# Gated attention rebuilt: decay matrix as one bf16 product of 94 rows, running maximum by a scan, tiles in an unrolled pipeline

## The reference, cut to what matters

```python
ig = x3 @ Wi + bi ; fg = x3 @ Wf + bf            # x3 = [q, k, v]; one value per position and head
log_f = log_sigmoid(fg)
cum = cumsum(log_f over positions)
log_D[s, t] = cum[s] - cum[t] + ig[t]  for t <= s, else -inf
max_log_D[s] = max over t of log_D[s, t]
D = exp(log_D - max_log_D)
C = (q @ k.T / 4) * D
Cn = C / (max(|C.sum(-1)|, exp(-max_log_D)) + 1e-6)
h = Cn @ v ; per head: h = (h - mean) * rsqrt(var + 1e-6) * ln_scale
x = x + h
```

## Time and profile before

| | us |
|---|---|
| median of 3 runs (lowest, highest) | 2200.45 (2195.76, 2201.08) |
| the profiled execution, its own time | 2195.36 |
| its span, first to last instruction | 2193.7 |
| the changed stage in it, first to last instruction | 761.3 to 1148.8 |
| mean granted TensorE clock over the span | 0.834 |

### The profile page before, as it was taken

The page is one execution under the profiler, slowest core; times in us unless marked ns, Lnnn a source line. Parts: engine busy times, 40 slices in busy tenths (PEclk is TensorE's granted clock), DMA queues, the critical chain, the costliest instruction groups (busy, mean ns, idle before and its releaser), DMA issues. The chain is left out here.

```text
span 2193.7 us, 34574 instructions
## 1 busy us (share of the span) xinstructions
PE 1514.8 (69%) x11413; PEld 938.5 (43%) x11458; DVE 1441.1 (66%) x2920; ACT 1114.8 (51%) x1540; POOL 570.7 (26%) x910
## 2 busy tenths in 40 slices
PE   3349999999399758787754575559999954776111
PEld 3326555555277634444421233335555542444000
DVE  6648888886245337667765999825555556775796
ACT  4517777777112124343444788723333334777454
POOL 3412333333200132322231344200010001111663
PEclk9999999999599969888985566569999977788555
DMA  5643555554200032112101000011010120000211
GB/s 168 196 108 86 136 131 131 134 131 95 80 1 0 4 75 48 43 45 62 34 7 60 0 1 1 1 39 35 25 34 23 27 82 20 1 1 1 48 48 39
DMA packets 94834, 120.62 MB, mean 55 GB/s; under 512 B 26128, under 2 KB 78552, under 8 KB 90108
## 3 DMA queue, kind: packets, MB, share of 16 engines
q1 hardware_dynamic: 94716, 119.12, 21.2%
HBM read 79.30 MB, written 22.09 MB: 46 GB/s over the span
## 5 line engine op out<-in xcount | busy, mean ns | idle before, releaser
L610 DVE TENSOR_REDUCE ratt_nmax<-ratt_psS 128x2 f32<-128x512 f32 x512 | 318.2, 683 | 92.9 <-PE ratt_psS L502 92.5
L576 ACT ACTIVATE ratt_E<-ratt_psT 128x1024 f32<-128x1024 f32 x256 | 255.0, 1023 | 106.0 <-PE ratt_psT L524 106.0
L502 PE MATMUL ratt_psS<-ratt_K,ratt_Q 72*128 72x256 bf16 x1024 | 204.3, 284 | 39.0 <-DMA ratt_K<-context_parts 33.6
L524 PE MATMUL ratt_psT<-ratt_Q,ratt_K 75*128 75x256 bf16 x1024 | 195.9, 275 | 5.5 <-DMA ratt_Q<-ratt_rows 5.2
L537 PE MATMUL ratt_psO<-ratt_E,ratt_V 128*32 128x256 f32 x2048 | 137.9, 387 | 0.7 <-ACT ratt_E L576 0.7
L502 PEld LDWEIGHTS ratt_psS<-ratt_K,ratt_Q 72*128 72x128 bf16 x1024 | 79.9, 99 | 135.1 <-issue 64.8
L524 PEld LDWEIGHTS ratt_psT<-ratt_Q,ratt_K 75*128 75x128 bf16 x1024 | 99.5, 98 | 23.5 <-DMA ratt_Q<-ratt_rows 5.6
L1355 PE MATMUL gatt_psA<-gatt_DA,gatt_same 128*128 128x512 f32 x128 | 89.3, 787 | 28.9 <-DVE gatt_DB L1240 25.3
L1174 POOL TENSOR_TENSOR gatt_DA<-gatt_own,gatt_a 128x1024 f32<-128x1024 f32 x32 | 61.6, 1937 | 143.8 <-PE gatt_psA L1358 90.6
L3302 PE MATMUL final_psT<-final_identh,final_Z 128*128 128x128 f16 x64 | 8.3, 310 | 110.4 <-ACT final_Z L3336 110.4
L1238 DVE TENSOR_REDUCE gatt_mx<-gatt_psA 128x16 f32<-128x1024 f32 x32 | 39.0, 1219 | 65.4 <-PE gatt_psA L1358 64.7
(11 more groups left out here) (461 smaller groups left out, 4000.3 us busy)
## 6 DMA issues: line engine op xcount, KB each, us to landing
ratt_Q<-z_parts SPq DMA_DIRECT2D x32, 576.0 KB
ratt_K<-context_parts SPq DMA_DIRECT2D x96, 192.0 KB
gatt_V<-in_ctx_dram SPq DMA_DIRECT2D x16, 512.0 KB, 6.2
z_parts<-prep_ZS SPq DMA_DIRECT2D x48, 128.0 KB, 2.7
context_parts<-prep_CS SPq DMA_DIRECT2D x48, 128.0 KB, 2.3
head_sums<-ratt_O SPq DMA_DIRECT2D x64, 72.0 KB
all_X<-in_x_dram SPq DMA_DIRECT2D x8, 512.0 KB
prep_C<-in_ctx_dram SPq DMA_DIRECT2D x8, 512.0 KB
```

The source lines that it names most:

```text
L502: mm = nc.tensor.matmul(psS[:, RING[h], c * D:(c + 1) * D], Q9[0:R, buf, h, k % 2, c * P:(c + 1) * P], K9[0:R, buf, h, k % 2, :], start=Tr ...
L524: mm = nc.tensor.matmul(psT[:, p % 2, e, c, :], K9[0:RM, buf, h, u, c * P:(c + 1) * P], Q9[0:RM, buf, h, u, :], start=True, stop=True)
L576: nc.scalar.activation(E[:, 2 * b + p // 2, 2 * (p % 2):2 * (p % 2) + 2], psT[:, p % 2], ACT.Exp, scale=SCALE).then_inc(exped, 1)
L610: nc.vector.tensor_reduce(nmax[:, k % 2, h, :], psS[:, RING[h]].rearrange("p (c t) -> p c t", c=2), AX.X, ALU.max, negate=True).then_inc(m ...
```

## The change

1. The diagonal spread on POOL, its f32 product, the separate mask product, the maximum over psA and the subtraction go. Instead a tile's exponent comes from one bf16 product per half of the heads, with 94 rows to contract (`decay`): 64 rows of an identity pattern against the mask, 24 rows for minus the running maximum of 8 heads in three bf16 parts, 6 rows for `a` of the two sequences in three bf16 parts. ACT's exponential reads psA and writes PB; DVE's `weigh` multiplies PB in place.
2. Per group PE transposes `a` to 64 partitions (group tile and head) x 128 positions (`turn_a`), DVE runs a maximum scan over each sequence (`running_maximum`), PE transposes the maximum back (`turn_maximum`, `take_maximum`), POOL splits `a` and minus the maximum into three bf16 parts (`split_rows`, five instructions on 64 x 256), SP writes them to DRAM in one DMA, waits for it, and reads them into the operands in five (`decay_rows`). These are double-buffered.
3. All engines run 44 unrolled slots (one per tile, 12 to fill and drain). In slot n = 4g + i, group g is prepared, tile t = n - 6 gets decay and exponential, tile t-1 is scored and weighed, tile t-2 is turned and multiplied by the values; the tail of group g-3 is done at i = 0, 1, 2.
4. The tail's Ln, Exp and Newton step become one POOL power on 128 x 64 (`power`); `tail` is 15 steps instead of 19. `sq` shares the memory of Z; `cen` is doubled. The gates read CT directly, so one DMA of 512 KB a group (`context`) goes. Keys are issued one half at a time, around `decay_rows` and the values' DMAs.

```diff
-                def spread_a(g, i):
-                    t = g * G + i
-                    pe.wait_ge(da_done, t + 1)
-                    pe.wait_ge(a_taken, t)
-                    for half in range(2):
-                        nc.tensor.matmul(psA[:, half, :], same[:],
-                                         DA[:, i % 2, half * HC:(half + 1) * HC, :].rearrange("p h t -> p (h t)"),
-                                         start=True, stop=False)
-                        mm = nc.tensor.matmul(psA[:, half, :], identb[:], mask[:].rearrange("p h t -> p (h t)"),
-                                              start=False, stop=True)
-                    mm.then_inc(a_spread, 1)
+                def decay(t):
+                    g, j = at(t)
+                    w = g % 2
+                    if j == 0:
+                        pe.wait_ge(rows_in[w], (g // 2 + 1) * ROWS_IN)
...
+                    if t > 0:
+                        pe.wait_ge(d_done, t)
+                    for c in range(KC):
+                        mm = nc.tensor.matmul(psA[:, c, :], LT[0:ROWS, w, j, c].rearrange("p u t -> p (u t)"),
+                                              R[0:ROWS, w, j, c].rearrange("p h t -> p (h t)"), start=True, stop=True)
+                    mm.then_inc(decayed, 1)
...
+                def decay_rows(g):
+                    w = g % 2
+                    sp.wait_ge(split, g + 1)
...
+                    sp.dma_start(rows_dram[w].rearrange("n p h t -> h n p t"), parts[:]).then_inc(rows_out, 16)
+                    sp.wait_ge(rows_out, g * 16 + 16)
...
+                    for p in range(3):
+                        sp.dma_start(LT[MX_ROW + p * HC:MX_ROW + (p + 1) * HC, w].rearrange(
+                            "h j c u t -> h (j c) (u t)"), rows_dram[w, 1, p].rearrange(
+                                "(x h) t -> h x t", h=HC)).then_inc(rows_in[w], 16)
+                    for u in range(2):
+                        for_u = rows_dram[w, 0].rearrange("p h (u t) -> u p h t", u=2)[u]
+                        sp.dma_start(R[A_ROW + 3 * u:A_ROW + 3 * u + 3, w].rearrange("p j c h t -> p (j c h) t"),
+                                     for_u).then_inc(rows_in[w], 16)
...
+                def power(g):
+                    pool.wait_ge(t_steps, g * TPER + 13)
+                    gp.tensor_tensor(tw[:, 9].rearrange("p j h -> p (j h)"), tw[:, 8].rearrange("p j h -> p (j h)"),
+                                     half[:], ALU.pow).then_inc(powered, 1)
...
+                for g in range(NG + 3):
                     if is_group(g + 1):
                         norm.on_pool(pool, g + 1)
+                    if is_group(g - 3):
+                        power(g - 3)
                     if is_group(g):
+                        split_rows(g)
+                    if is_group(g - 3):
+                        add(g - 3)
...
+                def running_maximum(g):
+                    step = Steps(dve, pair_steps, PPER, g)
+                    dve.wait_ge(a_turned, g + 1)
...
+                    step(v.tensor_copy(pair[:, 0], psG[0:GH, 0:P]))
+                    for u in range(2):
+                        x = pair[:, 0, u * L:(u + 1) * L]
+                        step(v.tensor_tensor_scan(pair[:, 2, u * L:(u + 1) * L], x, x, LOW, ALU.max, ALU.max))
+                    step(v.tensor_scalar(pair[:, 1], pair[:, 2], -1.0, None, ALU.mult))
...
+                for n in range(SLOTS):
+                    g, i = at(n)
+                    if i == 0:
+                        if is_group(g):
+                            front_gates(g)
+                        if is_tile(n - 7):
+                            weigh(n - 7)
+                        if is_group(g - 3):
+                            tail_centre(g - 3)
                     if i == 1:
+                        if is_group(g):
+                            front_logs(g)
+                        if is_tile(n - 7):
+                            weigh(n - 7)
+                        if is_group(g + 1):
+                            norm.take_stats(dve, g + 1)
+                        if is_group(g):
+                            front_sums(g)
+                        if is_group(g - 3):
+                            tail_variance(g - 3)
+                    if i == 2:
+                        if is_group(g):
+                            running_maximum(g)
+                        if is_tile(n - 7):
+                            weigh(n - 7)
+                        if is_group(g + 1):
+                            if is_group(g):
+                                dve.wait_ge(z_turned, g * KC + KC)
+                            norm.normalise(dve, g + 1, Z)
+                        if is_group(g - 3):
+                            tail_scale(g - 3)
                     if i == 3:
+                        if is_group(g):
+                            take_maximum(g)
+                        if is_tile(n - 7):
+                            weigh(n - 7)
...
+                for n in range(SLOTS):
+                    g, i = at(n)
+                    t = n - 6
+                    if is_group(g) and i == 1:
+                        running_sums(g)
+                    if is_tile(t):
+                        decay(t)
+                    if is_group(g) and i == 2:
+                        turn_a(g)
+                    if is_group(g) and i == 3:
+                        turn_maximum(g)
+                    if is_tile(t - 2):
+                        tg, tj = at(t - 2)
+                        heads.turn(pe, tg, tj)
+                    if is_group(g + 1) and i == 3:
+                        turn_z(g + 1, 0)
+                    if is_tile(t - 1):
+                        tg, tj = at(t - 1)
+                        heads.scores(pe, tg, tg % 3, tj)
+                    if is_group(g + 1) and i == 3:
+                        turn_z(g + 1, 1)
+                    if is_tile(t - 2):
...
+                        heads.values(pe, tg, tg % 2, tj)
+                    if is_group(g + 1) and i == 3:
+                        gates_of(g + 1)
...
+                for n in range(SLOTS):
+                    g, i = at(n)
+                    t = n - 6
+                    if is_group(g) and i == 0:
+                        softplus(g)
+                    if is_tile(t - 2):
+                        tg, tj = at(t - 2)
+                        heads.copy_turned(act, tg, tj)
+                    if is_tile(t):
+                        exp(t)
+                    if is_group(g + 1) and i == 3:
+                        query(g + 1, 0)
+                        query(g + 1, 1)
+                    if is_group(g - 3) and i == 0:
+                        tail(g - 3)
+                    if is_group(g - 1) and i == 1:
+                        place_values(g - 1)
+                    if is_tile(t - 2):
+                        take_output(t - 2)
```

More of the change, by code:

```diff
@@ L1062, in gated_attention @@
         lscale = s.sb("lscale", [P, D])
[L1063 to L1065 removed]
+        tri = s.sb("tri", [P, P])
         one = s.sb("one", [P, 1])
+        half = s.sb("half", [P, GH])
         Z = s.sb("Z", [P, G, D])
[L1068 removed]
         V2 = s.sb("V2", [P, BG, D])
@@ L1110, in _, with rows_of_context @@
                 c_dram = io["ctx_2048"].rearrange("b t d -> t b d")
-                def context(at):
-                    sp.dma_start(CG[:], CT[:, :, bass.ds(at, G * P)]).then_inc(cg_in, 16)
-                def rows_of_context(b0):
+                def rows_of_context(g):
                     for hp in range(2):
[L1117 to L1123, removed]
-                    if is_group(g + 1):
[L1125 to L1134, removed]
@@ new lines, in keys @@
+                def keys(g, half):
+                    after = g * G - 2 + 2 * half
+                    if after > 0:
+                        sp.wait_ge(heads.scored, after)
+                    for c in range(KC):
+                        for h in range(HC):
+                            rows = slice(h * DH, (h + 1) * DH)
+                            first = g * (G * P) + half * HG
+                            sp.dma_start(KX[rows, half, c, h, :], CT[rows, c, first:first + HG]).then_inc(
+                                heads.kx_in[half], 16)
@@ L1140, in _ @@
+                rows_of_context(0)
+                keys(0, 0)
+                keys(0, 1)
+                for g in range(NG):
+                    decay_rows(g)
+                    if g > 0:
+                        keys(g, 0)
+                    if is_group(g + 1):
+                        sp.wait_ge(v_copied, g * 2 + 2)
+                        rows_of_context(g + 1)
+                    if g > 0:
+                        keys(g, 1)
             @block.gpsimd
@@ new lines, in front_logs, with front_sums @@
+                def front_logs(g):
+                    dve.wait_ge(f_ln, g + 1)
+                    v.tensor_tensor(fw[:, 4], fw[:, 3], fw[:, 2], ALU.subtract).then_inc(f_steps, 1)
+                def front_sums(g):
```

(6 more changed lines are left out.)

423 lines of the change are left out of this document (190 added, 233 removed).

## The result

The kernel before took 2196.59 us (median of 5 runs beside the changed one, 2195.76 to 2201.08), the changed kernel 2213.69 us (5 runs, 2208.7 to 2218.6): a ratio of 1.0074, 95% interval 1.0059 to 1.0088. 2152 was forecast with "faster" at 0.74; the sign is wrong. The wide range of 2108 to 2222 holds the result only because it was drawn to reach the slow rival; the forecast's own range was 2128 to 2176. The profiled execution of the changed kernel has a span of 2216.9 us at a mean granted clock of 0.811 (before 0.834).

A forecast was written before the change was run, and what follows sets the result against it. No engine was full; one chain through a single psA bound the loop. Steady groups at 34.2 + 3 = 37.2 us plus the ends put the stage's end at 1100, 48.5 less: 2147, median 2152; own range 2128 to 2176, wide 2108 to 2222.

The forecast's parts named there:

- the slow rival: Tail's POOL power priced by its columns, 13.2 us for 64, outlasting what hides it: 2223 us in all, chance 0.18.
- I take 4, the geometric middle: Tail's POOL power on 64 columns: 4 us assumed, between about 1.2 (fixed start-up) and 13.2 (column by column).
- by the column: Rival: POOL's power costs 0.2 + 64 x 0.203 = 13.2 us, adding 71 in groups and tails: 2223, chance 0.18.
- The cover: DVE work between tail_variance and tail_scale that hides POOL's power: scan part 1.1, weigh 1.25, normalisation 3.5, together 5.9 us.
- a, PE slot 0: Steady group, start of the path: PE's decay 0.45, turn 0.93 and scores 1.77, together 3.2 us.
- b, DVE: Steady group, next on the path: DVE's weigh 1.25, tail_centre 3.0 and front_logs 0.25, 4.5 us; PE's running_sums waits.
- c, PE sums to scores: Steady group, PE behind front_logs: sums 0.26, decay, turn, scores and signals, 3.6 us.
- d, DVE: Steady group, DVE: two weighs, statistics 1.8, two short ones 0.5, tail_variance 3.6, scan part 1.1, together 9.5 us.
- e, DVE to turn_z: Steady group, DVE before PE's turn_z: normalisation 3.5 (bounds 1.6 and 5.2), tail_scale 1.5, take_maximum 0.25: 5.3 us.
- f, PE to the gates: Steady group, PE's last part: transposes, scores 1.8, values 1.1, gates 3.65, copies and signals 0.6, together 8.1 us.
- The first normalisation no longer waits for POOL's constants: Start of the stage: reason given for first gates about 4 us earlier, at 789 instead of 793.1.
- 37.2 against 40.7: Period of a steady group in us, forecast against the earlier trace's tail spacing: a yield of 3.5 a group.

The follow-up runs named there:

- power a product: Changed kernel with the tail's POOL power on 128 x 64 replaced by a multiplication, inverse root left out: 2159.38 us, ratio 0.9826 to the kernel before.
- both: Changed kernel with tail_scale moved behind the weighing of slot 3 and POOL's power made a multiplication: 2138.58 us, ratio 0.9722 to the kernel before.
- `tail_scale` late: Changed kernel with tail_scale moved from slot 2 to behind the weighing of slot 3, power kept: 2166.42 us, ratio 0.9842 to the kernel before.
- the root on ScalarE: Changed kernel with POOL's power replaced by Ln and Exp on ScalarE and a Newton step on VectorE: 2165.9 us, ratio 0.9866 to the kernel before.
- the fastest kernel: Changed kernel with tail_scale behind slot 3's weighing, front_logs in slot 0, start reordered, inverse root on ScalarE: 2112.81 us, ratio 0.962 to the kernel before.

## Why the prediction was wrong, point by point

**The step that failed first: "I take 4, the geometric middle" for the power.** It takes 10.55. The two bounds (1.2 and 13.2) held it, and the rival "by the column" had the mechanism. The middle was no reading: no row of the trace spoke for 4. By the rival's own terms 10.55 gives 5 x 4.65 + 3 x 6.55 = 43 us more, 2195, no change; 19 us are left. The rival's point from which it decides, about 11 us, was too high as well.

**The cover was 3.7 us, not 5.9.** It was made of a normalisation at 3.5; four of them took 1.37 (988.50). The shorter step shortened what hid the power by as much. The wait was 6.9 where the formula gives 4.65.

**What the waits cost TensorE: the clock was put too high.** The prediction lists `turn_z` and the gates as queued behind the power. It took 3 us a group for a lower clock, and TensorE's legs came out 8.3 longer than at its full-clock price. Leg by leg, from the sixth to the seventh gates in each trace:

| leg (us) | forecast | changed | power a product | both |
|---|---|---|---|---|
| a, PE slot 0 | 3.2 | 5.6 | 5.6 | 4.6 |
| b, DVE | 4.5 | 4.4 | 4.4 | 4.4 |
| c, PE sums to scores | 3.6 | 6.0 | 6.0 | 5.3 |
| d, DVE | 9.5 | 9.4 | 9.4 | 9.4 |
| e, DVE to turn_z | 5.3 | 10.7 | 3.9 | 2.3 |
| f, PE to the gates | 8.1 | 11.6 | 11.6 | 8.3 |
| sum | 34.2 + 3 | 47.8 | 40.9 | 34.3 |

VectorE's legs b and d are right to 0.1 us. TensorE's three legs (a, c, f) are 14.9 + 3 in the forecast and 23.2 in the trace, with or without the power. So even a power of 0.32 us leaves the period at 40.9 instead of 37.2: where 0.83 was taken for the clock, the steady groups had 0.73, and 0.75 with the product. When `turn_z` no longer waits behind `tail_scale`, the sum of 34.2 is met, by a shorter leg e against longer legs a and c.

**The start had the wrong sign.** "The first normalisation no longer waits for POOL's constants" misreads the diff: `norm.on_pool(0)` still stands last in POOL's program, with eight selections for two new bases ahead of it (4.7 us, for 2.7 us of old ones that are gone), and KX's zeros (3.5 us), which VectorE set ahead of its first statistics before, now stand behind the first normalisation. From the start of the stage the first gates come 4 us later instead of 4 earlier.

**A yardstick was mixed.** The 40.7 us of the earlier trace rows is a mean over steady and last tails. From gates to gates before had 44.4 us in its steady groups (176.2 / 4 = 44.1 over the four). The absolute sum was not touched by it, but "37.2 against 40.7" understated what a dense loop could gain.

**Two small slips in the sums.** The terms of the ends add to 312 us, not 311. A power of 0.3 us would take 3 x 3.7 = 11 us off the forecast by its own terms, not 9. Neither changes the verdict.

**Luck:** the end without the power took 86.3 us, where the forecast had 85.5. But the forecast held a power of 4 us in each of the last three tails; without it, it would have said about 74, so the rest of the end was put 12 us too short.

**Right:** the stall in front of `running_sums` ("about 3 us", 3.62; its removal gave 27 us); groups 0 to 2 roughly (77.5, 71.1); a scan at 0.29 (0.28); SyncE no bound. In the waits SyncE shows 14.5 us in 8 for its own write of the rows and no engine waits for the reads. The rows of the new product, the split and the scan follow. The product's mean of 0.47 us mixes the two clock levels: the two instructions of a tile took 0.60 us together at the granted clock of 1.00, and 1.04 at 0.50; the forecast had 0.45.
```profile
L1413 PE MATMUL gatt_psA<-gatt_R,gatt_LT 94*128 94x512 bf16 x64 | 24.2, 468 | 1.5 <-ACT gatt_PB L1475 1.5
...
L1201 POOL TENSOR_TENSOR gatt_rest<-gatt_rest,gatt_parts 64x256 f32<-64x256 f32 x8 | 5.3, 662 | 0.6
...
L1264 DVE TENSOR_TENSOR_SCAN gatt_pair<-gatt_pair 64x64 f32<-64x64 f32 x16 | 4.5, 282 | 0.6
```
The Trainium skill's rule cited there (GPSIMD Engine Reference, section 3.1: about 2.6 cycles an element) holds here for the product of 64 columns (0.32 us, its estimate 0.3) and not for the power, 33 times that.

**What stays open.** Why the period without the power is 35.4 us with `tail_scale` late (34.3 in two groups, 37.4 in the last) and 34.6 with the power was not tried. What sets TensorE's clock is open as well. A gap's length alone doesn't: with the root on ScalarE the scores behind a gap of 2.54 us took 1.94 us, and in the fastest kernel those behind a gap of 1.19 took 3.31. Last, 4 of the start's 12 us are not found again in the median.

## What to carry to other kernels

An operation whose cost is known at one width only is not priced by a middle: run the sum at both ends, and where they differ in sign, measure the operation first. The prediction did run both ends and gave the slow one 0.18; what it lacked was a reason for the middle. In an in-order queue look for what stands behind a wait, not at the wait: moving a 0.2 us copy ahead of a blocked instruction gave 35 us, while the blocked instruction waited as long as before. And a stall of TensorE can cost more than its length: here the scores behind the gap took 3.68 us instead of 1.94. Read the clock of the stretch in the trace, since the gap's length didn't tell it.

## What was not expected of the hardware

- POOL's power: 0.56 us for one column, 10.55 for 64, the same on 64 and 128 partitions; a product of 64 columns took 0.32.
- The power left VectorE alone, and some of POOL's other work did not. Four normalisations took 1.37 us beside the power; beside the split, in the kernel without it, 2.14; and in the fastest kernel a VectorE instruction of 64 columns that takes 0.20 alone took 2.37 beside POOL's addition of 1024 columns (start, duration, instruction):
```profile
948.93 2.36 POOL L1217 TENSOR_TENSOR all_X<-all_X,gatt_cen 128x1024 f32<-128x1024 f32 x1
...
948.97 2.37 DVE L1239 TENSOR_SCALAR gatt_fw<-gatt_gates 128x64 f32<-128x64 f32 x1
```
